# Layer 3's values and their weight product in the return stage of layer 2's routed rows

## The reference, cut to what matters

```python
def _L2_ffn_ref(x, w12, w3, shared_w1, shared_w2, shared_w3, router_w, expert_bias):
    ...
    shared = jax.nn.silu(xf @ shared_w1.T) * (xf @ shared_w2.T) @ shared_w3.T
    scores = jax.nn.sigmoid(xf @ router_w.T)
    _, top_idx = jax.lax.top_k(scores + expert_bias, TOP_K)
    ...
    h = jax.nn.silu(h1) * h2 * gates[:, :, None]
    routed = jnp.einsum('teh,edh->td', h, w3)
    return (shared + routed).reshape(b, s, d)

def _L3_xattn_ref(hidden_states, hidden_states_multi, Wg, Wq, Wk, Wv, Wo, W1, b1, W2, b2):
    ...
    logits = x[:, 0, :] @ Wg
    top_idx = jnp.argmax(logits, axis=-1)
    ...
    q = jnp.einsum('bsh,hd->bsd', x, Wq)
    k = jnp.einsum('bsh,hd->bsd', xm, Wk)
    v = jnp.einsum('bsh,hd->bsd', xm, Wv)
    attn = jax.nn.softmax(jnp.einsum('bqd,bkd->bqk', q, k) * scale, axis=-1)
    e0 = jnp.einsum('bqk,bkd->bqd', attn, v) @ Wo
    e1 = jax.nn.gelu(x @ W1 + b1, approximate=False) @ W2 + b2
    sel0 = (top_idx == 0)[:, None, None]
    final_hidden_states = jnp.where(sel0, e0, e1)
    return final_hidden_states
...
    x = x + _L2_ffn_ref(_layernorm(x, axis=-1), ...)
    x = x + _L3_xattn_ref(_layernorm(x, axis=-1), ctx_1024, ...)
```

## Time and profile before

| | us |
|---|---|
| median of 3 runs | 1528.09 (1527.57 to 1533.8) |
| the profiled execution | 1529.01 |
| its span | 1527.0 |
| TensorE busy | 1397.2 (92%) |
| VectorE busy | 896.7 (59%) |
| ScalarE busy | 693.7 (45%) |
| GpSimd busy | 353.0 (23%) |
| mean granted clock of TensorE | 0.946 of full speed |

### The profile page before, as it was taken

The page is one execution under the profiler, slowest core; times in us unless marked ns, Lnnn a source line. Parts: engine busy times, 40 slices in busy tenths (PEclk is TensorE's granted clock), DMA queues, the critical chain, the costliest instruction groups (busy, mean ns, idle before and its releaser), DMA issues. The chain is left out here.

```text
span 1527.0 us, 24679 instructions
## 1 busy us (share of the span) xinstructions
PE 1397.2 (92%) x8362; PEld 1122.4 (74%) x8362; DVE 896.7 (59%) x1704; ACT 693.7 (45%) x1134; POOL 353.0 (23%) x365
## 2 busy tenths in 40 slices
PE   5799999799999999999999699999989798993994
PEld 4544444588898888889888587888877687882893
DVE  6778887744555555555555843444466657544456
ACT  5366667343443443344343165555543354452431
POOL 2102224311221222122121122333310056331000
PEclk8889999889999999999999799999999989996996
DMA  6802220211111111111110114555422134323000
GB/s 226 254 15 51 53 64 16 62 41 51 41 41 62 41 41 57 46 41 42 61 41 7 49 43 117 145 143 142 124 81 83 41 118 142 94 91 107 1 1 27
DMA packets 63799, 110.83 MB, mean 73 GB/s; under 512 B 10331, under 2 KB 39517, under 8 KB 62845
## 3 DMA queue, kind: packets, MB, share of 16 engines
q1 hardware_dynamic: 61869, 104.93, 23.3%
q0 software_dynamic: 1872, 5.13, 0.9%
HBM read 90.91 MB, written 18.97 MB: 72 GB/s over the span
## 5 line engine op out<-in xcount | busy, mean ns | idle before, releaser
L1217 DVE TENSOR_TENSOR hidden_l<-silu_l,up_l 128x512 f32<-128x512 f32 x128 | 88.1, 688 | 219.9 <-ACT silu_l L1157 219.9
L1157 ACT ACTIVATE silu_l<-gate_l 128x512 f32<-128x512 f32 x128 | 76.6, 599 | 308.5 <-PE up_l L75 308.5
L851 DVE TENSOR_REDUCE maxima<-a_scores 128x1 f32<-128x512 f32 x256 | 164.6, 686 | 41.4 <-PE a_scores L790 40.0
L73 PE MATMUL out_l<-dn_hi_l,h_hi_l 128*128 128x256 f32 x576 | 164.0, 285 | 7.6 <-DVE h_lo_l L2472 7.6
L75 PE MATMUL out_l<-dn_hi_l,h_lo_l 128*128 128x256 f32 x576 | 163.6, 284 | 0.0
L74 PE MATMUL out_l<-dn_lo_l,h_hi_l 128*128 128x256 f32 x576 | 163.6, 284 | 0.0
L818 ACT ACTIVATE probs<-b_scores 128x1024 f32<-128x1024 f32 x128 | 131.1, 1024 | 67.0 <-PE b_scores L747 64.9
L1189 POOL TENSOR_TENSOR gu_lo_l<-gu_raw_l,gu_hi_l 128x1024 fp32r<-128x1024 f32 x31 | 74.4, 2399 | 298.8 <-ACT gu_hi_l L1149 298.8
L1241 DVE SCALAR_TENSOR_TENSOR x_sb<-out_l,cw,x_sb 128x256 f32<-128x256 f32 x256 | 109.0, 478 | 22.4 <-PE out_l L75 18.1
L73 PEld LDWEIGHTS out_l<-dn_hi_l,h_hi_l 128*128 128x128 f32 x576 | 110.9, 192 | 11.0 <-ACT h_hi_l L2365 6.2
L73 PE MATMUL gate_l<-xnT_hi_n,gu_hi_l 128*128 128x512 f32 x288 | 115.2, 400 | 1.7 <-ACT xnT_hi_n L220 1.2
(11 more groups left out here) (451 smaller groups left out, 3382.6 us busy)
## 6 DMA issues: line engine op xcount, KB each, us to landing
gu_raw_l<-w_units SPq DMA_DIRECT2D x32, 512.0 KB, 3.9
spread_l<-cw_rows SPq DMA_DIRECT2D x64, 256.0 KB, 3.8
dn_raw_l<-w_units SPq DMA_DIRECT2D x32, 256.0 KB, 2.6
k_stack<-k_stacks SPq DMA_DIRECT2D x8, 768.0 KB, 5.7
staged_l<-w_experts SPq DMA_DIRECT2D x24, 256.0 KB, 2.7
up_raw_l<-w SPq DMA_DIRECT2D x40, 128.5 KB, 3.4
dn_raw_l<-w SPq DMA_DIRECT2D x40, 128.0 KB, 2.0
phi_a<-fside SPq DMA_DIRECT2D x8, 512.0 KB, 3.2
```

Source lines behind the costliest of these rows:

```text
L73: pe.matmul(out, lhs[0], rhs[0], start=start, stop=False, skip_group_check=True)
L851: dve.tensor_reduce(maxima[k // 16][:, i // 2, i % 2:i % 2 + 1], a_scores[:, k % 2, :], X, ALU.max).then_inc(a_read, 1)
L1157: act.activation(silu[:, q % 2, :], gate[:, q % 2, :], ACT.Silu).then_inc(silu_done, 1)
L1217: dve.tensor_tensor(hidden[:, q % 2, :], silu[:, q % 2, :], up[:, q % 2, :], ALU.mult).then_inc(hidden_done, 1)
```

## The change

Values and the product of their two weights move from the front stage of layer 3 to the return stage before it. What the edits are:

- `v_hi` and `v_lo` of layer 3 are allocated before the expert stage, and that stage's inputs and tiles become parts of them: `xnT_hi` and `xnT_lo` lie in `v_hi`, `h_hi`, `h_lo` and the gate and up tiles in `v_lo` (these now as 2 x 2 x 128 in place of 512 in a row).
- In the expert stage SyncE loads Wv and Wo (512 KB) into the storage of `hidden`, after the first three block loads and after waits for the last hidden tiles. GpSimd copies the high half and subtracts for the low one, ahead of its first scatter of results.
- GpSimd's waits for the scatters leave the end of the expert stage; SyncE waits for them at the start of the return stage.
- The return stage gets the weight product, its two halves, and eight value tiles with theirs. VectorE makes four low halves of values before its first sum, and one more in each round.
- The front stage loses those nine tiles and one load. Its copies on ScalarE are in another order: the weights of `w12_3` and `wg3` come ahead of the normalised rows.

```diff
 def l2_sparse_phase(nc, g, d):
-        gu_hi, gu_lo = several("gu_hi", [P, 2, KC, FS], F32R), several("gu_lo", [P, 2, KC, FS], F32R)
+        quarters = [g.v_lo[:, 8 + 2 * i:10 + 2 * i, :].rearrange("p k (w f) -> p w k f", w=2) for i in range(4)]
+        gu_hi, gu_lo = quarters[0:2], quarters[2:4]
...
-        h_hi, h_lo = sb("h_hi", [P, T], F32R), sb("h_lo", [P, T], F32R)
+        h_hi, h_lo = [g.v_lo[:, 4 * i:4 * i + 4, :].rearrange("p c e -> p (c e)") for i in range(2)]
...
+        pair_raw = hidden[:, :, :].rearrange("p w (k f) -> p w k f", k=KC)
+        g.pair_hi, g.pair_lo = [g.v_hi[:, 8 + 4 * i:12 + 4 * i, :].rearrange("p (w k) f -> p w k f", w=2) for i in range(2)]
+        g.scattered2 = [(scattered[i], 16 * len(range(i, NB2, OUTS))) for i in range(OUTS)]
...
                 for b in range(BLOCKS):
                     load_block(b)
+                sp.wait_ge(h_hi_done, 2 * N)
+                sp.wait_ge(h_lo_done, 2 * N)
+                sp.dma_start(pair_raw, d["wqkvo3"][:, 2:4, :, :]).then_inc(pair_loaded, 16)
...
+                pool.wait_ge(pair_loaded, 16)
+                pool.wait_ge(gu_done, 2 * N)
+                pool.tensor_copy(g.pair_hi, pair_raw).then_inc(pair_split, 1)
+                pool.wait_ge(pair_split, 1)
+                pool.tensor_tensor(g.pair_lo, pair_raw, f32(g.pair_hi), ALU.subtract).then_inc(pair_split, 1)
+                pool.wait_ge(pair_split, 2)
                 for b in range(NB2):
...
-                for i in range(OUTS):
-                    pool.wait_ge(scattered[i], 16 * len(range(i, NB2, OUTS)))
...
 def l2_return_phase(nc, g):
...
             def _(sp):
+                for done, count in g.scattered2:
+                    sp.wait_ge(done, count)
...
+            @block.tensor
+            def _(pe):
+                for c in range(KC):
+                    f = slice(c * P, (c + 1) * P)
+                    for k in range(KC):
+                        last = mm3(pe, product[:, c, :], (g.pair_hi[:, 0, k, f], g.pair_lo[:, 0, k, f]),
+                                   (g.pair_hi[:, 1, k, :], g.pair_lo[:, 1, k, :]), c == 0 and k == 0, k == KC - 1)
+                last.then_inc(product_done, 1)
+                pe.wait_ge(w_hi_done, 1)
+                pe.wait_ge(w_lo_done, 1)
+                for m in range(TILES):
+                    if m >= 4:
+                        pe.wait_ge(v_lo_done, m - 3)
...
+            @block.scalar
+            def _(act):
+                act.wait_ge(product_done, 1)
+                act.activation(w_hi[:, :, :], product[:, :, :], ACT.Copy).then_inc(w_hi_done, 1)
+                for m in range(TILES):
+                    act.wait_ge(values_done, m + 1)
+                    act.activation(v_of(g.v_hi, m), acc[:, m % 4, :], ACT.Copy).then_inc(v_hi_done, 1)
...
             @block.vector
             def _(dve):
+                def low(m):
+                    dve.wait_ge(v_hi_done, m + 1)
+                    dve.tensor_tensor(v_of(g.v_lo, m), acc[:, m % 4, :], f32(v_of(g.v_hi, m)), ALU.subtract).then_inc(v_lo_done, 1)
...
-                sum_parts(0)
-                for i in range(PIECE):
-                    add_parts(i)
-                    if i + 1 < PIECE:
-                        sum_parts(i + 1)
+                def stats(i):
                     dve.wait_ge(added, i + 1)
                     take_stats(dve, g, (2 * i, 2 * i + 1))
 
+                dve.wait_ge(w_hi_done, 1)
+                dve.tensor_tensor(w_lo[:, :, :], product[:, :, :], f32(w_hi[:, :, :]), ALU.subtract).then_inc(w_lo_done, 1)
+                EARLY = TILES - PIECE
+                for m in range(EARLY):
+                    low(m)
+                for i in range(PIECE):
+                    sum_parts(i)
+                    add_parts(i)
+                    low(EARLY + i)
+                    stats(i)
...
 def l3_front_phase(nc, g, d):
-        tiles = [("weight", 1), ("value", 0), ("value", 1), ("weight", 0)] + [("value", m) for m in range(2, CT // P // 2)]
+        tiles = [("weight", 0)]
         tiles += [("hidden", (fc, h)) for h in range(2) for fc in range(KC)]
...
-                sp.dma_start(pair_raw[:, 2:4, :, :], d["wqkvo3"][:, 2:4, :, :]).then_inc(pairs_loaded[1], 16)
-                sp.dma_start(pair_raw[:, 0:2, :, :], d["wqkvo3"][:, 0:2, :, :]).then_inc(pairs_loaded[0], 16)
+                sp.dma_start(pair_raw[:, :, :, :], d["wqkvo3"][:, 0:2, :, :]).then_inc(pair_loaded, 16)
...
                 norm.root(act)
-                split_pair(1)
-                norm.high(act, 0)
-                split_pair(0)
-                high(0)
-                norm.high(act, 1)
+                split_pair()
                 act.wait_ge(mlp_loaded, 32)
                 act.activation(mlp_hi[:, :, :, :], mlp_raw[:, :, :, :], ACT.Copy).then_inc(mlp_hi_done, 1)
                 act.activation(wg_hi[:, :, :], wg_raw[:, :, :], ACT.Copy).then_inc(mlp_hi_done, 1)
+                norm.high(act, 0)
+                norm.high(act, 1)
+                high(0)
...
 def four_layers(nc, d, out_dram, upto=99):
+        g.v_hi, g.v_lo = [values.enter_context(nc.sbuf_tensor(f"v_{h}_l3", [P, CT // P, D], F32R)) for h in ("hi", "lo")]
+        with ExitStack() as experts:
+            g.xnT_hi, g.xnT_lo = [g.v_hi[:, 8 * i:8 * i + 8, :].rearrange("p (k c) e -> p k (c e)", k=KC) for i in range(2)]
```

79 lines of the change are left out of this document (43 added, 36 removed).

## The result

The changed kernel takes 1524.08 us (median of 13 runs, 1520.12 to 1526.31), the kernel before 1529.33 us in the same comparison (13 runs, 1524.95 to 1534.61). The ratio is 0.9957 with an interval of 0.9945 to 0.997: **faster by 0.43%**, some 6.6 us of 1529.33 (the two medians lie 5.3 apart). The forecast was 1525.8, a gain of 2.3: the time came within 1.7 us of it, from a base that is 1.2 us higher here than the median it started from, and the gain was more than twice as large. The profiled execution took 1522.15 us with a span of 1520.2, 6.9 and 6.8 less than before.

A forecast was written before the change was run, and what follows sets the result against it. A VectorE chain, then a TensorE chain, each on the path, divided by a barrier. + 9.7 (return) - 13.2 (front) + 1.2 (experts) = - 2.3 us; 1529.01 - 2.3 = 1526.7, 0.9 less for the median: 1525.8; eight in ten 1518 to 1532.

The forecast's parts named there:

- the return stage's + 9.7: Return stage, with product and eight value tiles added: ends at 1405.2, 9.7 us later than 1395.46.
- the front stage's - 13.2: Front stage of layer 3, without nine tiles: 32.7 us instead of 45.9, a gain of 13.2 us (11.5 to 14.8).
- The start of the stage: Release of the return stage after the last scatter: 1378.1 at the earliest, 1382.9 as before.
- S = 1383.1: TensorE's first matmul of the return stage, S, placed at 1383.1 by taking the release as late as before.
- the rival of a fixed price: End of expert stage: 3.8 us counted from the last instruction, release at 1381.5, time 1524.3 us; chance 0.15.
- the choice between the bounds: Return stage's release: 1378.1 or 1382.9; the later taken, since 3.8 us after the landing is more than the wait explains.
- F: End of the return stage, forecast at 1405.2, from which the front stage's times are counted.
- S + 22.1: Return stage's end after TensorE's first matmul: fourth low half ends at 11.7, four rounds take 10.3, tail 0.1 us.
- The rival of a slow clock: Return stage: value tiles at the low clock take about 2.6 us for 1.44; time 1531.5 us; chance 0.10.
- the 1.6 us set down for low hidden tiles: Front stage: hidden tiles run 3.3 us at half speed, losing 1.6 us (0 to 3.3).
- The experts' blocks: Expert stage: GpSimd's subtraction may hold VectorE's block 2 target up to 2.3 us; 1.2 us lost taken (0 to 2.4).
- The later stages: Phases after layer 3's front stage: the change costs nothing there that a row shows.

The follow-up runs named there:

- the two kernels with the wait alone: Changed kernel with the scatter waits back on GpSimd: 1527.47 us; kernel before with only those waits moved to SyncE: 1526.22 us.
- the kernel with the early weights: Changed kernel with the front stage's weights loaded in the return stage and split there by GpSimd: 1523.06 us, ratio 0.9951 to the kernel before.
- that with one stage: Changed kernel with expert and return stage made one, no barrier between: 1513.4 us, ratio 0.9903 to the kernel before.
- the extra matmuls: 60 unread matmuls in the front stage, added to the kernel with merged stages, early weights and ScalarE making their high halves: 1510.75 us, ratio 0.9869.

## Why the prediction was right, and where it was not

The forecast of 1525.8 us was right to 1.7 us, and the large terms, the return stage's + 9.7 and the front stage's - 13.2, had the right mechanism. The gain of 2.3 us is a small difference between them, and there the misses below show: it was more than twice as large.

**The start of the stage: wrong.** The forecast took the upper bound, S = 1383.1, "since 3.8 us is more than the wait explains". S was 1381.52. The explanation was right (closing the stage is what costs), but the price counts from GpSimd's last instruction or wait, so that moving the wait gives back what lies between a scatter's instruction and its landing. That was the rival of a fixed price, with 1381.5 and a chance of 0.15, and the two kernels with the wait alone show it in both directions: 1.65 us. The step that failed is the choice between the bounds: nothing in the rows spoke for the count from the landing against the count from the last instruction, and the layer 0 barrier cited there told only what closing costs without scatters. The trace of the kernel before had more than those rows: its DRAIN starts only when the wait is over, so the 3.2 us are no part of the wait, and moving the wait lets it start sooner.

**The return stage: a term too small, for the clock.** F was to be S + 22.1 and was 1405.38, S + 23.9. The rounds were sized well (2.57 us; 1394.97 to 1397.56 is 2.59), and VectorE never waited between them. The fourth low half ended at S + 13.5 and not S + 11.7: the price was read from the front stage, where sixteen transposes went before the product, and the clock rose in the pause behind it, ahead of the first value tile; here it rose only at 1390.1, one and a half value tiles later. The rival of a slow clock needed more than two low tiles to decide. This 1.8 and the 1.6 us of the earlier start (1383.1 to 1381.52) cancel, so that F came at 1405.38 where 1405.2 was forecast. That is luck.

**The front stage: right in mechanism, 2.5 us too small.** The first hidden tile did wait for GpSimd's low half of w12_3, and from it to the end it was 20.4 us (20.3 forecast). It began at F + 9.8 and not F + 10.8, since the load of wg3 let ScalarE start at F + 5.7 and not at F + 6.8: with one load less before it, it was issued 0.5 us sooner, which the forecast left out, and it landed 4.6 us after its issue, not 5.2. And the 1.6 us set down for low hidden tiles were not paid, as the clock rose within the product, at 1414.0. That was the lower end of that term.

**The experts' blocks: right in mechanism, half the size.** The pair landed at about 1318.0 and not 1317.0, so the target operations of blocks 2 and 3 were held for 0.60 and 0.75 us, not block 2's alone for up to 2.3. They end with GpSimd's instructions, at 1319.07 and 1321.54 where these end at 1319.05 and 1321.53. Expected 1.2, lost about 0.5.

The Trainium skill (SBUF — State Buffer, Who interferes with whom) says that whichever of the two comes first has the shared ports for its whole instruction. Here and in the kernel with the early weights (a sum of 2.31 us under a subtraction of 2.40) the traces agree, and the low halves of values, which read one input from the accumulators, stayed at 0.68 to 0.69 beside GpSimd, as the page states for one SBUF input.

**The later stages: taken for nothing, gave 1.0 us.** The attention, from G to its successor's first instruction, took 63.85 us before and 62.76 after. The same stretch in the kernel before, the kernel after, and the one with ScalarE's old order (PE clock third from the end):

```profile
1441.36:1505.21 63.85, 56.94 (x352) 51.01 (x352) 29.31 (x56) 19.17 (x26) 0.00 (x0) 0.92 0.00 1
...
1435.58:1498.34 62.76, 55.83 (x352) 50.33 (x352) 29.31 (x58) 19.16 (x26) 0.00 (x0) 0.95 0.00 1
...
1449.61:1509.31 59.70, 52.77 (x352) 47.28 (x352) 29.30 (x57) 19.17 (x26) 0.00 (x0) 1.00 0.00 1
```

Its length follows the clock: with no time at the lower level it was 59.7 us, with 3.4 us of it 61.2 and 61.3, with about 6.8 us 62.6 to 62.8, and with 10 us (as before) 63.9 to 64.6, over all thirteen traces. Before, the low time lay at its start (to 1447.9) and from 1499.1 to 1502.5, after from 1485.7 to 1489.1 and from 1492.5 to 1495.9. Each low stretch began in, or at most 1.6 us behind, a pause of TensorE of 2.4 to 2.8 us. The attention has three such pauses, one at its start (2.79 us before, 2.80 after) and two inside, and some were followed by a low stretch and some not: none of the three in the kernel with ScalarE's old order, all three in that with one stage. So this is no effect of the change that the runs show, and about 1 us of the profiled 6.8 may be luck. What decides which pause is followed by a low stretch stays open; the extra matmuls covered the first pause and not the two inside.
